# Expert tiles of a mixture-of-experts layer: two products on 128 stationary columns, or on four column tiles of 32

## The chip, the cores and the metric

One NeuronCore of a Trainium2 chip runs the whole program. The metric is the device time of one execution in microseconds, the median of several runs; lower is better. TensorE does the matrix products and transposes, ScalarE (ACT) and VectorE (DVE) take results out of the accumulators (PSUM), GpSimd (POOL) issues the gathers and scatters, and the queue SP issues nearly all other transfers.

## The reference

The input is 8 streams of 512 tokens with 128 features. Four parts follow one another, each added to its input: a four-layer attention encoder with dense feed-forward layers, a mixture of experts, a rotary attention layer, and the same mixture of experts again. The mixture is the part that the change touches:

```
top_v, top_i = jax.lax.top_k(routing_logits, TOP_K)          # 2 of 8 experts per token
...
h = gelu(jnp.einsum('bnd,edf->bnef', x, W1) + b1)             # D = 128, F = 512
y = jnp.einsum('bnef,efd->bned', h, W2) + b2
out = jnp.einsum('bne,bned->bnd', comb, y)
```

All of it is float32.

## The kernel before

The kernel doesn't compute all experts for all tokens. Tokens are sorted by chosen expert: each normalised token is scattered to two places of a list in memory (`x_rows`), each expert's part of the list is padded to a multiple of 256 rows, and the list is worked through in **tiles** of 256 rows of one expert. The first mixture is **round 0**, the second **round 1**; each has 46 tiles, in two groups of streams (23 and 23 in round 0, 31 and 15 in round 1).

One tile runs as follows. SP loads the expert's pack (both weights and biases, 578 KB) and the tile's 256 rows into one of six buffers. TensorE transposes the rows in two pieces of 128 (`rows_to_columns`, L779), ScalarE copies them out of PSUM (L937). `up` (L794) forms the four pieces of the hidden layer: the stationary operand is a 128 x 128 piece of W1, the moving one the 256 columns of the tile. ScalarE applies gelu with the bias (L952). `down` (L804) forms the result: for each half of 128 rows, four products with 128 stationary and 128 moving columns are accumulated. VectorE adds the bias (L1393), and SP stores the rows in `y_rows`. GpSimd later gathers each token's two rows (L1560), and VectorE adds them up with their weights (L1186).

The order on each engine is written out by hand. In a tile's first half TensorE does `up` of tile i and then the transposes of tile i+1; in its second half `down` of tile i-1. Between the halves, `tiles_order` puts other work: first the tail of the attention layer before (`tail`, 2 positions a half tile in round 0, 1.5 in round 1), and in round 0, once the first streams are combined, the head of the rotary attention layer (`head`, 2.45 positions a half tile). Where neither is left, the stream of TensorE is `up`, transposes, `down`, `up`, ... alone.

Nearly all products of the attention and dense layers go through the helper `mm4` (L482 to L485): it splits the 128 stationary columns into four column tiles of 32, issues one matmul for each, and writes 32 partitions of the result with each. In the profile these carry the line of the helper, L484, and the shape `128*32` (rows * columns of the stationary operand). The score products of the attention, L604 and L612, are written as column tiles as well, and L650 uses 9 columns of each. The transposes (L491, L668, L674, L779), the routing products and, before the change, both products of an expert tile use the full array, `128*128`. A product of float32 data appears in the trace as two pairs of weight load and matmul.

Of the kernel before, what the change touches and what calls it, by code (L numbers as in the profile page):

```python
# [27 lines left out]
P = 128  # L28
D = 128
# [5 lines left out]
FT = 4  # L35
# [35 lines left out]
TILE = 256  # L71
# [9 lines left out]
DEEP = 6  # L81
# [15 lines left out]
def hybrid_kernel(nc, x, apack, fpack, final, bpack, mpack, b2e, w1e, w2e,  # L97
                  alibi, rope, out, part_scr):
    ctx = ExitStack()
    with ctx:  # L100
# [3 lines left out]
        def sem(name):  # L104
            return ctx.enter_context(nc.semaphore(name))
# [34 lines left out]
        W1 = [pack[n][:, 0:FT * P] for n in range(DEEP)]  # L140
        W2 = [pack[n][:, FT * P:2 * FT * P].rearrange("p (f d) -> p f d", f=FT) for n in range(DEEP)]
# [5 lines left out]
        xcols = [rest[:, 768 + TILE * n:768 + TILE * (n + 1)] for n in range(2)]  # L147
        hT = [rest[:, 1280 + FT * TILE * n:1280 + FT * TILE * (n + 1)].rearrange("p (f t) -> p f t", f=FT) for n in range(2)]
# [54 lines left out]
        bankX, bankH = [bank[0], bank[4]], [bank[1:3], [bankPV, bankR]]  # L203
# [67 lines left out]
        eh_ready = sem("eh_ready")  # L271
# [195 lines left out]
        def beside(round_, i):  # L467

            return round_ == 0 and i >= FIRST[0]

        def one_bank(round_, i):

            return round_ == 0 and i >= FIRST[0] - 3

        def bank_of_results(round_, i):
            return bankY[0 if one_bank(round_, i) else (round_ * ETILES + i) % 2]

        @block.tensor
        def _(pe):
            mm = nc.tensor.matmul  # L480

            def mm4(out, stationary, moving, start=True, stop=True):  # L482
                for c in range(0, P, 32):
                    last = mm(out[c:c + 32], stationary[:, c:c + 32], moving, start=start, stop=stop)  # L484
                return last  # L485
# [296 lines left out]
            def up(round_, i):  # L782
                n = round_ * ETILES + i
                pe.wait_ge(exT_ready, n + 1)
                if i == FIRST[0] and round_ == 0:
                    jobs = ENC + round_ * JOBS
                    pe.wait_ge(slots_ready, JOBS * (round_ + 1))
                    pe.wait_ge(ot_done, QUADS * jobs)
                    pe.wait_ge(x_added, 2 * jobs - 1)
                    pe.wait_ge(f_added, 2 * ENC - 1)  # L790
                for ft in range(FT):
                    if n >= 1 and ft % 2 == 0:
                        pe.wait_ge(egelu_done, FT * (n - 1) + ft + 2)
                    mm(bankH[beside(round_, i)][ft // 2][:, (ft % 2) * TILE:(ft % 2 + 1) * TILE], W1[i % DEEP][:, ft * P:(ft + 1) * P],  # L794
                       xcols[n % 2], start=True, stop=True).then_inc(eh_ready, 1)

            def down(round_, i):
                n = round_ * ETILES + i
                pe.wait_ge(egelu_done, FT * (n + 1))
                if n >= 2:  # L800
                    pe.wait_ge(ey_added, n if one_bank(round_, i) else n - 1)
                for h in range(2):
                    for ft in range(FT):
                        last = mm(bank_of_results(round_, i)[:, h * D:(h + 1) * D], hT[n % 2][:, ft, h * P:(h + 1) * P],  # L804
                                  W2[i % DEEP][:, ft, :], start=(ft == 0), stop=(ft == FT - 1))
                last.then_inc(ey_ready, 1)

            def tile(round_, i, half_tile):
                if half_tile == 0:
                    if i == 0:  # L810
                        rows_to_columns(round_, 0)
                    up(round_, i)
                    if i + 1 < ETILES:
                        rows_to_columns(round_, i + 1)
                else:
                    if i >= 1:
                        down(round_, i - 1)
                    if i == ETILES - 1:
                        down(round_, i)
# [1050 lines left out]
```

## Time and profile before

| | |
|---|---|
| median of 3 runs | 2507.29 us (2502.47 to 2508.13) |
| profiled execution, first to last instruction | 2558.5 us; the page gives no time of its own beside the span |
| TensorE matmul busy | 2237.2 us (87%) |
| TensorE weight load busy | 1405.0 us (55%) |
| VectorE, ScalarE, GpSimd busy | 1764.9, 1442.5, 1042.2 us |
| mean granted TensorE clock | 0.933 |
| L794 (`up`), L804 (`down`): matmul busy | 188.4 and 185.9 us |

The share of a whole span is an average over stages. The tiles of round 0 lie between about 1575 and 1850 us, those of round 1 between 2310 and 2517 us; for those stretches the views by window and in order of time are of more use. In the timeline, a group's length reaches from its first start to its last modelled end; since matmuls are pipelined, the next group starts before that end, so the cost of a group is read from start to start.

### The profile page before, as it was taken

Reading aid. Unit: us, or ns where it says so; the run is one execution under the profiler, and the core shown is the slowest. Engines: PE = TensorE matmul, PEld = TensorE weight load, DVE = VectorE, ACT = ScalarE, POOL = GpSimd, SP = SyncE. Lnnn points to the kernel's source line nnn. Section 1 sums busy time; section 2 is a strip of 40 time slices with the busy share of each in tenths; the row PEclk is TensorE's granted clock in tenths of the full one; section 3 lists DMA queues with packets and bytes.
Section 4 is the critical chain, followed back from the end, with each engine's and each line's share of the span. In section 5 each row is a group of like instructions: output and inputs, shape, how many; then the busy total and the mean of one; then the engine's idle time right before and its main releaser. Section 6 shows DMA issues by size and latency. Waiting matters only on the chain.

```text
span 2558.5 us, 102575 instructions
## 1 busy us (share of the span) xinstructions
PE 2237.2 (87%) x44398; PEld 1405.0 (55%) x44398; DVE 1764.9 (69%) x5525; ACT 1442.5 (56%) x2646; POOL 1042.2 (41%) x1261
## 2 busy tenths in 40 slices
PE   2689999999999999999998888887888777888983
PEld 1345565656555656565555445786644444437872
DVE  6777888787878888888888774224677767852212
ACT  0257777777777777777755555342244434554441
POOL 6233434343434343434455554333244554452135
PEclk9789999999999999999988889999998888889997
DMA  4244433333433433433222203575522221206774
GB/s 117 82 137 118 128 117 123 114 124 113 127 117 116 130 107 119 125 121 110 78 68 69 83 25 107 166 227 161 150 62 66 62 68 60 61 18 194 218 211 111
DMA packets 162531, 288.76 MB, mean 113 GB/s; under 512 B 28504, under 2 KB 116312, under 8 KB 160344
## 3 DMA queue, kind: packets, MB, share of 16 engines
q1 hardware_dynamic: 153696, 264.23, 33.9%
q0 software_dynamic: 8384, 17.97, 2.6%
q8 instruction: 350, 5.73, 0.9%
q14 instruction: 101, 0.83, 0.1%
HBM read 227.33 MB, written 95.96 MB: 126 GB/s over the span
## 4 chain that ended last, share of the span: by engine, by line
PE 67%; DVE 14%; ACT 6%; issue 4%; POOL 3%; DMA 2%; another core or an unknown queue 2%; SPq 2%; POOLq 0%; ACTq 0%; DVEq 0%
PE bank L484 25%; PE bank L650 11%; PE bank L604 10%; PE bank L794 5%; DVE mx L1287 4%; PE bank L804 4%; PE bank L668 3%; PE bank L491 2%; ACT L915 1%; PE bank L612 1%; ACT big L885 1%; DVE xs L1186 1%; ACT fhT L915 1%; ACT OT L891 1%
## 5 line engine op out<-in xcount | busy, mean ns | idle before, releaser
L885 ACT ACTIVATE big<-bank 128x512 f32<-128x512 f32 x1600 | 900.2, 597 | 599.6 <-PE bank L484 518.5
L1287 DVE TENSOR_REDUCE mx<-bank 128x16 f32<-128x512 f32 (+1 forms) x1440 | 895.0, 653 | 290.5 <-PE bank L612 242.2
L1583 POOL TENSOR_SCALAR_AFFINE_SELECT big<-big 128x768 f32<-128x768 f32 (+1 forms) x640 | 397.6, 644 | 853.5 <-ACT big L885 853.4
L484 PE MATMUL bank<-QS,KS 99*32 99x128 bf16 (+3 forms) x10240 | 655.5, 312 | 32.4 <-ACT big L885 21.4
L604 PE MATMUL bank<-KS,QS 96*32 96x512 bf16 (+15 forms) x10240 | 592.9, 294 | 67.7 <-DVE mx L1287 40.0
L650 PE MATMUL bank<-big,V 128*9 128x512 f32 (+3 forms) x5120 | 445.3, 451 | 19.8 <-POOL big L1583 9.4
L604 PEld LDWEIGHTS bank<-KS,QS 96*32 96x32 bf16 x10240 | 249.9, 99 | 307.9 <-issue 155.1
L484 PEld LDWEIGHTS bank<-QS,KS 99*32 99x32 bf16 x10240 | 222.9, 99 | 201.0 <-ACT big L885 86.9
L612 PE MATMUL bank<-mask_a,ident_b 128*32 128x64 bf16 (+1 forms) x5760 | 309.6, 196 | 1.7 <-issue 1.7
L952 ACT ACTIVATE big<-bank,big 128x256 f32<-128x256 f32 x368 | 150.6, 471 | 247.7 <-PE bank L794 206.7
L650 PEld LDWEIGHTS bank<-big,V 128*9 128x9 f32 x5120 | 131.5, 92 | 167.9 <-issue 103.7
L1393 DVE TENSOR_TENSOR big<-bank,big 128x256 f32<-128x256 f32 x92 | 39.0, 424 | 255.9 <-PE bank L804 184.7
L794 PE MATMUL bank<-big 128*128 128x256 f32 x736 | 188.4, 401 | 24.2 <-ACT big L937 18.4
L804 PE MATMUL bank<-big 128*128 128x128 f32 x1472 | 185.9, 280 | 13.1 <-issue 10.0
L612 PEld LDWEIGHTS bank<-mask_a,ident_b 128*32 128x32 bf16 x5760 | 167.6, 99 | 38.1 <-issue 33.4
L804 PEld LDWEIGHTS bank<-big 128*128 128x128 f32 x1472 | 175.6, 195 | 18.5 <-issue 15.8
L794 PEld LDWEIGHTS bank<-big 128*128 128x128 f32 x736 | 140.1, 201 | 50.1 <-ACT big L937 21.4
L1568 POOL TENSOR_TENSOR resid<-qk,parts 128x512 f32<-128x512 f32 x80 | 96.5, 1206 | 170.8 <-DVE parts L1244 170.8
L1540 POOL DMA_INDIRECT x_rows<-xnR,slots x128 | 126.2, 986 | 59.9 <-issue 31.3
L484 PE MATMUL bank<-xnT,fp_sb 128*32 128x512 f32 x1024 | 133.1, 612 | 11.7 <-ACT fhT L915 11.6
L668 PE MATMUL bank<-ident,OT 128*128 128x128 f32 x640 | 109.4, 296 | 34.3 <-DVE attn L1328 31.6
L484 PE MATMUL bank<-fp_sb,fhT 128*32 128x128 f32 x4096 | 130.3, 273 | 0.2 <-ACT fhT L915 0.2
(216 smaller groups left out, 2732.0 us busy)
## 6 DMA issues: line engine op xcount, KB each, us to landing
big<-e_pack SPq DMA_DIRECT2D x92, 578.0 KB
QS<-part_scr SPq DMA_DIRECT2D x480, 96.0 KB
KS<-part_scr SPq DMA_DIRECT2D x480, 96.0 KB
part_scr<-parts SPq DMA_DIRECT2D x80, 384.0 KB
x_rows<-in_alibi SPq DMA_DIRECT2D x47, 384.0 KB, 4.8
y_rows<-in_alibi SPq DMA_DIRECT2D x47, 384.0 KB, 5.1
big<-x_rows SPq DMA_DIRECT2D x92, 128.0 KB
y_rows<-big SPq DMA_DIRECT2D x92, 128.0 KB
```

The lines of the kernel that those rows point to most:

```text
L484: last = mm(out[c:c + 32], stationary[:, c:c + 32], moving, start=start, stop=stop)
L604: mm(bk[h * SUB:(h + 1) * SUB, col:col + w], Q[0:ROW_MAX, 4 * quad + h, i * SUB:(i + 1) * SUB], K[0:ROW_MAX, 4 * quad + h, 0:w], start=(co ...
L612: last = mm(blocks[h * SUB:(h + 1) * SUB], ident_b[:, 0:SUB], mask, start=False, stop=True)
L650: last = mm(bankPV[32 * h:32 * h + HD + 1, kt * P:T], V[(b + j) % 3][:, kt, 4 * g + h, :], Pq[g % 2][:, h, KT_COL[kt]:KT_COL[kt] + T - kt ...
L668: last = nc.tensor.transpose(bankR[:, g * P:(g + 1) * P], OT[:, g, t * P:(t + 1) * P], ident[:])
L794: mm(bankH[beside(round_, i)][ft // 2][:, (ft % 2) * TILE:(ft % 2 + 1) * TILE], W1[i % DEEP][:, ft * P:(ft + 1) * P], xcols[n % 2], start= ...
L804: last = mm(bank_of_results(round_, i)[:, h * D:(h + 1) * D], hT[n % 2][:, ft, h * P:(h + 1) * P], W2[i % DEEP][:, ft, :], start=(ft == 0) ...
L885: A(dst, src, ACT.Exp).then_inc(exp_done, 1)
L952: A(hT[n % 2][:, ft, :], bankH[beside(round_, i)][ft // 2][:, (ft % 2) * TILE:(ft % 2 + 1) * TILE], ACT.Gelu, bias=B1[i % DEEP][:, ft:ft + ...
L1287: v.tensor_reduce(mx[:, quad, k, 0:w], src, axis=AX.X, op=ALU.max).then_inc(a_used, 1)
L1540: g.indirect_dma_start(out=x_rows, out_offset=bass.IndirectOffsetOnAxis(ap=slots[:, S % JOBS, c:c + 1], axis=0), in_=xnR[:, S % 2, c % TT, ...
L1583: g.affine_select(out=blocks, in_=blocks, compare_op=ALU.is_ge, fill=0.0, base=0, pattern=[[0, n], [1, P]], channel_multiplier=-1).then_in ...
```

## The change

Both products of an expert tile go through `mm4`: instead of one matmul with 128 stationary columns, four with 32 each are issued one after another. The moving operands, the accumulation over the hidden pieces, the waits and the semaphore increments are the same (the increment is on the last of the four). The transposes of the tile are unchanged.

```
-                    mm(bankH[beside(round_, i)][ft // 2][:, (ft % 2) * TILE:(ft % 2 + 1) * TILE], W1[i % DEEP][:, ft * P:(ft + 1) * P],
-                       xcols[n % 2], start=True, stop=True).then_inc(eh_ready, 1)
+                    mm4(bankH[beside(round_, i)][ft // 2][:, (ft % 2) * TILE:(ft % 2 + 1) * TILE], W1[i % DEEP][:, ft * P:(ft + 1) * P],
+                        xcols[n % 2]).then_inc(eh_ready, 1)
...
-                        last = mm(bank_of_results(round_, i)[:, h * D:(h + 1) * D], hT[n % 2][:, ft, h * P:(h + 1) * P],
-                                  W2[i % DEEP][:, ft, :], start=(ft == 0), stop=(ft == FT - 1))
+                        last = mm4(bank_of_results(round_, i)[:, h * D:(h + 1) * D], hT[n % 2][:, ft, h * P:(h + 1) * P],
+                                   W2[i % DEEP][:, ft, :], start=(ft == 0), stop=(ft == FT - 1))
```

The helper, which was there before:

```
            def mm4(out, stationary, moving, start=True, stop=True):
                for c in range(0, P, 32):
                    last = mm(out[c:c + 32], stationary[:, c:c + 32], moving, start=start, stop=stop)
                return last
```

## Rows read from the trace of the kernel before

**Rows 1.** Windows, L794 alone: window, its length, busy us (entries), clock, DMA share, GB/s.

```profile
1735.00:1850.00 115.00, 34.47 (x128) 25.09 (x128) 0.93 0.56 161
2310.00:2515.00 205.00, 91.34 (x368) 68.50 (x368) 0.97 0.70 204
```

**Rows 2.** Windows: busy us (entries) of PE, PEld, DVE, ACT, POOL; clock; DMA share; GB/s.

```profile
1735.00:1850.00 115.00, 101.06 (x1129) 76.81 (x1127) 61.98 (x160) 31.62 (x81) 34.33 (x34) 0.93 0.56 161
2310.00:2515.00 205.00, 186.29 (x1294) 168.75 (x1287) 42.98 (x178) 92.17 (x236) 57.18 (x59) 0.97 0.70 204
2410.00:2460.00 50.00, 50.00 (x352) 46.64 (x351) 5.76 (x14) 25.20 (x67) 2.47 (x3) 1.00 0.81 230
```

**Rows 3.** The chain that ended last, 2250 to 2560 us, shares by line.

```profile
by line: PE bank L794 27.1%; PE bank L804 22.2%; another core or an unknown queue 6.7%; PE bank L650 4.8%; POOL xnR L1560 4.5%; PE bank L484 4.3%; ACT big L885 3.6%; issue 3.6%; ACT big L952 3.4%; PE bank L779 2.9%; POOL fp_sb L1560 2.1%; P
```

**Rows 4.** Timeline of PE, one tile of round 1: start us, length us, engine, line, instruction.

```profile
2414.74 1.89 PE L794 MATMUL bank<-big 128*128 128x256 f32 x8
2416.46 0.38 PE L779 MATMUL bank<-ident,big 128*128 128x128 f32 x2
2416.68 1.95 PE L804 MATMUL bank<-big 128*128 128x128 f32 x16
2418.47 1.89 PE L794 MATMUL bank<-big 128*128 128x256 f32 x8
```

**Rows 5.** Timeline of PE, dense layer of the encoder in column tiles.

```profile
1005.43 1.92 PE L484 MATMUL bank<-xnT,fp_sb 128*32 128x512 f32 x16 [0.17 <-ACT fhT L915]
1007.17 0.29 PE L604 MATMUL bank<-KS,QS 96*32 96x256 bf16 x4
...
1008.18 1.94 PE L484 MATMUL bank<-fp_sb,fhT 128*32 128x128 f32 x64
1009.94 0.40 PE L604 MATMUL bank<-KS,QS 96*32 96x512 bf16 x4
```

**Rows 6.** Timeline of PE, rotary layer: column tiles, full-array transposes, column tiles.

```profile
1907.49 1.07 PE L484 MATMUL bank<-xnT,bp_sb 128*32 128x512 f32 x8 [0.70 <-DVE rtmp L1261]
1908.49 0.66 PE L668 MATMUL bank<-ident,OT 128*128 128x128 f32 x4
1909.08 0.29 PE L604 MATMUL bank<-KS,QS 96*32 96x256 bf16 x4
```

**Rows 7.** Timeline of PE, round 0: a tile between positions of the head.

```profile
1802.84 0.21 PE L612 MATMUL bank<-mask_a,ident_b 128*32 128x64 bf16 x4
1802.98 1.99 PE L794 MATMUL bank<-big 128*128 128x256 f32 x8
1804.81 0.38 PE L779 MATMUL bank<-ident,big 128*128 128x128 f32 x2
1805.12 0.40 PE L604 MATMUL bank<-KS,QS 96*32 96x64 bf16 x8
...
1806.48 0.20 PE L612 MATMUL bank<-mask_a,ident_b 128*32 128x64 bf16 x4
1806.62 2.05 PE L804 MATMUL bank<-big 128*128 128x128 f32 x16
1808.60 0.40 PE L604 MATMUL bank<-KS,QS 96*32 96x128 bf16 x8
1808.83 0.20 PE L612 MATMUL bank<-mask_a,ident_b 128*32 128x64 bf16 x4
1808.86 0.39 PE L604 MATMUL bank<-KS,QS 96*32 96x160 bf16 x8
```

**Rows 8.** Waits, 1655 to 1735 us: who waited for whom, us in total, times, longest.

```profile
POOL fp_sb L1560 <- DMA y_rows<-big: 28.1, 1, 28.1
```

**Rows 9.** The page, its first line.

```profile
span 2558.5 us, 102575 instructions
```

**Rows 10.** Windows of 10 us, columns as in rows 2.

```profile
190.00:200.00 10.00, 9.72 (x321) 7.12 (x313) 7.15 (x28) 6.61 (x12) 2.44 (x4) 1.00 0.81 202
1800.00:1810.00 10.00, 10.00 (x162) 7.80 (x162) 9.53 (x22) 1.92 (x5) 3.51 (x4) 1.00 0.82 219
```

## The prediction

> **What bounds the kernel now.** I read the stage windows first, to find where the changed lines run. L794 (first product of an expert tile) and L804 (second) leave 8 and 16 entries a tile. All 46 tiles of the second round lie in 2310 to 2515 us (368 entries of L794); of the 46 of the first round 16 lie in 1735 to 1850 us (128 entries), so 30 before that [rows 1]. The reader should see two kinds of stretch. In 2310 to 2515 us TensorE is busy 186.3 of 205 us, and from 2410 to 2460 it is busy 50.00 of 50.00 us at granted clock 1.00 (2.4 GHz), while the DMA share is 0.81 [rows 2]. The chain that ended last confirms it for 2250 to 2560 us: L794 and L804 hold 27.1% and 22.2% of it [rows 3]. So in the second round TensorE's own stream sets the pace; ScalarE, VectorE and the loads fit beside it.
>
> The timeline of one tile there shows what the stream consists of [rows 4]: start to start, 1.72 us for the first product (8 entries: four products, each in two passes because the data is f32), 0.22 us for the two transposes L779, 1.79 us for the second product (16 entries). Sum 3.73 us a tile, no gaps. A change helps only if it shortens these three numbers or the joints between them.
>
> **The change part by part.** Each matmul on 128 stationary columns becomes four on 32. A tile had 8 + 2 + 16 = 26 pairs of weight load and matmul; it will have 32 + 2 + 64 = 98. No wait, DMA or semaphore increment is added: the increment sits on the last of the four.
>
> *Streaming.* The dense layers already run this form with f32, so the price is in the trace. Two dense first-layer products of 512 columns (16 entries on 32 stationary columns) stream as many columns as the four of 256 in a tile: start to start 1.74 us [rows 5], against 1.72. The dense second layer has 64 entries of 128 columns in 1.76 us [rows 5], exactly the number and shape that a tile's second product will have, against 1.79. Up and down together: 3.50 against 3.51. The form itself gains and loses nothing (-0.01 us).
>
> *The joints.* The transposes stay on the full array, so each tile's stream now goes column tiles, full, column tiles. Such a joint can be read elsewhere: a 512-column f32 product in column tiles ahead of four full transposes takes 1.00 us to the next start instead of 1.74/2 = 0.87, so +0.13; the four transposes then take 0.59 us to the next column tile instead of the 0.43 that twice a tile's two come to, so +0.16 [rows 6]. Round trip 0.29 us. Nearer in place, but without the entry, is the exit from two L779 transposes to a column tile in the first round: 0.31 instead of 0.22, +0.09 [rows 7]. Entry 0.13 and exit 0.09 give the lower bound 0.22; 0.29 is the upper. I take 0.27, nearer to the upper because only that row has both halves around one short group. With the -0.01 above a tile alone costs +0.26 us (bounds 0.21 and 0.28): 3.73 becomes 3.99 us.
>
> *Where joints are saved.* From 1735 to 1850 us the first attention work of the next layer, in column tiles, is woven into both halves of a tile. There the tile pays now [rows 7]: entry to L794 0.14 us after the mask matmuls instead of about 0.03, +0.11, and L794 itself 1.83 instead of 1.72, +0.11; exit after L779 +0.09; entry to L804 again +0.11; L804 to the next column tile 1.98 instead of 1.79, +0.19. Sum 0.61 us. After the change only the transposes are left as a joint, 0.27: a saving of 0.34 us for each tile woven so. I count 26 such crossings from column tiles to full array in that part, two a tile, so 13 of its 16 tiles; the other 3 behave like lone tiles.
>
> *The sum.* Second round: 46 x 0.26 = +12.0 us, all on the path by [rows 2, 3]. First round before 1735 us: 30 tiles x 0.26 = +7.8 us, but the end of that part hangs on a gather that waited 28.1 us for stored rows [rows 8], so some is hidden behind it; I take +5. The woven part: -13 x 0.34 + 3 x 0.26 = -3.6 us; TensorE is busy 101.1 of 115 us there [rows 2], VectorE and the loads end several of its waits, so I take half, -1.8. Together +15 us, rounded down to +14 because the tail of the first round has some full-array neighbours that don't pay twice. The profiled execution spans 2558.5 us [rows 9], 51 us more than the 2507.3 us median of the three runs; the page gives no other time of its own for it, and the sum of differences is carried over to the median unchanged: 2507.3 + 14 = **2521 us** (2572 on the profile's span).
>
> Bounds of this case: 46 x 0.21 + 0 - 13 x 0.39 = +4.6 us if everything ahead of 1735 us is hidden and the woven part counts in full; 46 x 0.28 + 30 x 0.28 - 0 = +21.3 us if it is the reverse. So 2512 to 2529.
>
> The Trainium skill (TensorEngine Tiling (Array Packing), Key Properties) says that a change of tiling mode drains the array. Taken as a full drain, an estimate from [rows 4] is the tail by which a group outlasts the start of the next (1.89 against 1.73 us), so 0.16 a crossing and 0.33 a round trip, 0.32 a lone tile; the same four terms would then come to some +19 us in place of +14. The trace has the drain, with 0.29 at most, so it comes out a little cheaper than that.
>
> **The rivals.**
>
> *The crossings cost nothing around so short a group.* If the loads for the two transposes go in while the last column tiles still stream, the lone tile stays at 3.72 us and the woven tiles gain their full 0.61 us: 76 x -0.01 - 13 x 0.61 = -8.7 us, 2499 us, faster. It decides below about 0.05 us a round trip (76 x 0.05 = 3.8 against 8.7). For it: no row shows two transposes with column tiles on both sides. Against it: every entry and every exit that I found costs 0.09 to 0.16 [rows 6, 7]. Chance 0.05.
>
> *The loss is swallowed.* TensorE idles 18.7 of the 205 us of the second round [rows 2]. If those pauses end at times set by transfers, a later TensorE finds them shorter, and the second round loses perhaps a third of its 12 us, the first nothing, with the saving of 3.6 in full: about 2508 us, no change. For it: the DMA share of 0.81. Against it: in 2410 to 2460 us, the stretch with the highest share, TensorE never waits. Chance 0.13.
>
> *Issue or instruction supply becomes the bound.* A tile has 98 pairs where it had 26, about 246 in 10 us at 3.99 us a tile. In the tile stretches the most seen in 10 us is 162 pairs, with TensorE busy 10.00 [rows 10]; were that a ceiling, a tile would take 98/16.2 = 6.05 us, 2.3 us more, and 76 of them +176 us: 2683. Against it: early in the kernel 321 pairs went through in 10 us at the same DMA share, 0.81 and 0.82 [rows 10]. Chance 0.02 for this, and some 0.04 for small pauses of it that bring the total to 2530 to 2545.
>
> The Trainium skill (TensorE: Matmul & The Clock Gate, section "Wait — 56ns, not 53.3ns?") states about 62 ns per matmul where microcode issues it; 98 x 0.062 = 6.08 us a tile by that, the same outcome. The trace disagrees here: 64 pairs in 1.76 us are 27 ns each [rows 5].
>
> **How the numbers follow.** Crossings as priced: 0.76; swallowed 0.13; free crossings 0.05; issue 0.06. A measurement of this kernel tells about 0.2% (5 us) from no change. Slower by more: 0.76 x 0.95 + 0.06 = 0.78; within: 0.04 + 0.13 = 0.17; faster: 0.05. The range runs from 2508 (the swallowed case at its edge) to 2530 (the upper bound of the likeliest); left out are the free crossings, issue, and a part of the swallowed case, under 2 in 10.
>
> **What would show it.** In the profile after, the lone tile of the second round should go 1.74 + 0.13 us from first product to transposes, 0.31 to 0.36 us from transposes to second product, 1.76 us to the next tile: period 3.94 to 4.01 us. The products appear at the line inside the helper (L484) with 32 columns, 2944 and 5888 matmuls. Between 1735 and 1850 us the tiles should get shorter by about 0.3 us. The clock granted should stay at 1.00 in the dense part. Wrong would be: a period of 3.73 or less (crossings free), a period above 4.1 with TensorE waiting for nothing that the profile shows (issue), or a longer period with the same end, pauses shrunk (swallowed).

## The result and the profile after

| | before | after |
|---|---|---|
| median of 5 runs | 2507.29 us (2502.47 to 2508.14) | 2522.88 us (2519.50 to 2530.20, but for one run) |
| ratio of after to before | | 1.0067, 95% interval 1.0050 to 1.0085 |
| span of the profiled execution | 2558.5 us | 2520.3 us |

The kernel became slower: by 0.67% in the ratio, and by 15.6 us between the medians, where +14 us (2521 us) was forecast. One of the five runs after, 2912.70 us at a granted clock of 0.73 where the others have 0.93 to 0.94, was disturbed and is left out of the ratio.

The spans of the two profiles go the other way, so stages can't be read off them. The first profile of the kernel before holds pauses in which several engines stand still; a second profile of the same kernel (run e0 below) spans 2506.7 us, and stages are compared with that one. First the page of the changed kernel, then the same lines of e0:

```profile
span 2520.3 us, 115823 instructions
PE 2224.5 (88%) x51022; PEld 1332.6 (53%) x51022; DVE 1774.0 (70%) x5525; ACT 1442.9 (57%) x2646; POOL 1043.7 (41%) x1261
q8 instruction: 402, 6.59, 1.1%
```

```profile
span 2506.7 us, 102575 instructions
PE 2210.1 (88%) x44398; PEld 1392.3 (56%) x44398; DVE 1772.0 (71%) x5525; ACT 1442.8 (58%) x2646; POOL 1042.4 (42%) x1261
q8 instruction: 350, 5.73, 1.0%
```

TensorE has 6624 more pairs of weight load and matmul, 92 x 72 as counted in the prediction; nothing else has changed in number. The products of the tiles now stand at the helper's line, in the counts forecast; their busy time is 183.0 and 181.6 us against 183.6 and 182.9 in e0, so the form itself costs nothing:

```profile
L484 PE MATMUL bank<-big 128*32 128x256 f32 x2944 | 183.0, 390 | 1.1 <-ACT big L937 1.1
L484 PE MATMUL bank<-big 128*32 128x128 f32 x5888 | 181.6, 275 | 1.8 <-DVE big L1393 1.4 <-issue 0.4
```

The timeline of PE for a lone tile of the second round answers to [rows 4]. `down` and `up` follow each other at one line, so they are merged (96 entries):

```profile
2401.25 0.44 PE L779 MATMUL bank<-ident,big 128*128 128x128 f32 x2
2401.61 3.68 PE L484 MATMUL bank<-big 128*32 128x128 f32 x96
2405.22 0.44 PE L779 MATMUL bank<-ident,big 128*128 128x128 f32 x2
2405.59 3.68 PE L484 MATMUL bank<-big 128*32 128x128 f32 x96
```

Start to start: 0.36 to 0.37 us from the transposes to `down` (0.22 before), 3.61 us for `down` and `up` (3.51 before), period 3.98 us (3.73 before). Both additions lie at the two joints. The load side shows what is lost there. In e0 the weight load of a group starts ahead of its first matmul and hides behind the group before: 0.21 us ahead for the transposes (2402.06 against 2402.27 us) and 0.11 us for `down` (2402.38 against 2402.49):

```profile
2402.06 0.36 PEld L779 LDWEIGHTS bank<-ident,big 128*128 128x128 f32 x2
2402.38 1.86 PEld L804 LDWEIGHTS bank<-big 128*128 128x128 f32 x16
```

After the change it starts only with the matmul, 2401.24 against 2401.25 us and 2401.61 against 2401.61:

```profile
2401.24 0.20 PEld L779 LDWEIGHTS bank<-ident,big 128*128 128x128 f32 x2 [0.41 <-issue]
2401.61 3.20 PEld L484 LDWEIGHTS bank<-big 128*32 128x32 f32 x96 [0.17 <-ACT big L952]
```

The gelu (L952) that the second line names had ended at 2398.2 us for the tile in question, so ScalarE isn't what held that load. The idle 0.4 us before the transposes' load stands in each of 32 tiles between 2330 and 2460 us; e0 has no such wait there.

In the same window TensorE is busy without a gap in both kernels, at granted clock 1.00 (first e0, then after), so neither the clock nor a wait for another engine explains anything there:

```profile
2330.00:2460.00 130.00, 130.00 (x915) 121.14 (x914) 29.57 (x112) 67.09 (x175) 40.12 (x41) 1.00 0.83 239
```

```profile
2330.00:2460.00 130.00, 130.00 (x3221) 94.43 (x3217) 27.79 (x109) 61.70 (x162) 32.63 (x34) 1.00 0.81 232
```

A woven tile, as in [rows 7]:

```profile
1795.63 1.90 PE L484 MATMUL bank<-big 128*32 128x256 f32 x32
1797.46 0.44 PE L779 MATMUL bank<-ident,big 128*128 128x128 f32 x2
1797.83 0.40 PE L604 MATMUL bank<-KS,QS 96*32 96x64 bf16 x8
...
1799.22 1.92 PE L484 MATMUL bank<-big 128*32 128x128 f32 x64
1800.97 0.39 PE L604 MATMUL bank<-KS,QS 96*32 96x128 bf16 x8
```

Its parts are 1.83, 0.37 and 1.75 us, 3.95 together. In [rows 7] they were 1.83, 0.31 and 1.98 with 0.11 us of entry ahead of each product, 4.34. It saves 0.39 us.

The stages can be cut where VectorE adds the bias of a tile (L1393): first tile of the first round, tile 29, last tile of that round, first and last of the second. First e0, then after:

```profile
1576.17 0.42 DVE L1393 TENSOR_TENSOR big<-bank,big 128x256 f32<-128x256 f32 x1 [0.95 <-PE bank L804]
1724.14 0.42 DVE L1393 TENSOR_TENSOR big<-bank,big 128x256 f32<-128x256 f32 x1 [1.19 <-PE bank L804]
1830.22 0.42 DVE L1393 TENSOR_TENSOR big<-bank,big 128x256 f32<-128x256 f32 x1 [2.21 <-PE bank L804]
2293.28 0.42 DVE L1393 TENSOR_TENSOR big<-bank,big 128x256 f32<-128x256 f32 x1 [3.26 <-PE bank L804]
2465.79 0.42 DVE L1393 TENSOR_TENSOR big<-bank,big 128x256 f32<-128x256 f32 x1 [1.36 <-PE bank L804]
```

```profile
1578.91 0.42 DVE L1393 TENSOR_TENSOR big<-bank,big 128x256 f32<-128x256 f32 x1 [1.09 <-PE bank L484]
1733.16 0.42 DVE L1393 TENSOR_TENSOR big<-bank,big 128x256 f32<-128x256 f32 x1 [0.98 <-PE bank L484]
1836.79 0.42 DVE L1393 TENSOR_TENSOR big<-bank,big 128x256 f32<-128x256 f32 x1 [2.16 <-PE bank L484]
2297.04 0.42 DVE L1393 TENSOR_TENSOR big<-bank,big 128x256 f32<-128x256 f32 x1 [3.67 <-PE bank L484]
2480.47 0.42 DVE L1393 TENSOR_TENSOR big<-bank,big 128x256 f32<-128x256 f32 x1 [1.27 <-PE bank L484]
```

| stretch | e0 | after | difference | forecast |
|---|---|---|---|---|
| first round, first tile to tile 29 | 148.0 | 154.3 | +6.3 | +5 |
| first round, tile 29 to the last (woven) | 106.1 | 103.6 | -2.4 | -1.8 |
| second round, first to last tile | 172.5 | 183.4 | +10.9 | +12.0 |

The rest of the 13.6 us between the spans, -1.2 us, lies in stretches without a tile, where the two executions differ by up to 3 us in either direction.

### The profile page after: what moved, and what is told of

It reads as the page before. It is cut to its first block, busy times and chain, and to the rows that moved or that the text cites. A ratio compares the mean times of both kernels' runs of the same rounds, so it can differ in the third digit from the quotient of the medians.

```text
span 2520.3 us, 115823 instructions
## 1 busy us (share of the span) xinstructions
PE 2224.5 (88%) x51022; PEld 1332.6 (53%) x51022; DVE 1774.0 (70%) x5525; ACT 1442.9 (57%) x2646; POOL 1043.7 (41%) x1261
## 4 chain that ended last, share of the span: by engine, by line
PE 64%; DVE 16%; POOL 5%; ACT 5%; issue 4%; DMA 4%; SPq 2%; POOLq 0%; ACTq 0%; DVEq 0%
PE bank L484 33%; PE bank L650 11%; PE bank L604 10%; DVE mx L1287 5%; PE bank L668 3%; PE bank L491 2%; ACT L915 2%; PE bank L612 1%; POOL x_rows L1540 1%; ACT big L885 1%; DMA KS<-part_scr 1%; DVE xs L1186 1%; DMA y_rows<-big 1%; PE bank L779 1%; ACT OT L891 1%
## 5 line engine op out<-in xcount | busy, mean ns | idle before, releaser
L484 PE MATMUL bank<-QS,KS 99*32 99x128 bf16 (+3 forms) x10240 | 647.4, 311 | 21.4 <-ACT big L885 16.2
L604 PE MATMUL bank<-KS,QS 96*32 96x512 bf16 (+15 forms) x10240 | 586.1, 293 | 86.1 <-DVE mx L1287 46.3
L650 PE MATMUL bank<-big,V 128*9 128x512 f32 (+3 forms) x5120 | 437.5, 451 | 20.3 <-POOL big L1583 14.3
L484 PE MATMUL bank<-big 128*32 128x128 f32 (+1 forms) x8832 | 352.2, 314 | 2.9 <-DVE big L1393 1.4
L484 PEld LDWEIGHTS bank<-big 128*32 128x32 f32 x8832 | 250.2, 111 | 74.7 <-issue 13.7
L952 ACT ACTIVATE big<-bank,big 128x256 f32<-128x256 f32 x368 | 151.0, 470 | 231.5 <-PE bank L484 231.3
L1393 DVE TENSOR_TENSOR big<-bank,big 128x256 f32<-128x256 f32 x92 | 38.8, 423 | 225.0 <-PE bank L484 203.9
L668 PE MATMUL bank<-ident,OT 128*128 128x128 f32 x640 | 109.4, 296 | 32.7 <-DVE attn L1328 30.2
L1449 POOL TENSOR_TENSOR rstd<-veps,mhalf 128x4 f32<-128x4 f32 x80 | 81.1, 1014 | 106.4 <-DVE veps L972 103.6
L1560 POOL DMA_INDIRECT fp_sb<-y_rows,slots x80 | 77.2, 964 | 106.1 <-DVE big L1393 49.4
```

The lines of the kernel that those rows point to most:

```text
L604: mm(bk[h * SUB:(h + 1) * SUB, col:col + w], Q[0:ROW_MAX, 4 * quad + h, i * SUB:(i + 1) * SUB], K[0:ROW_MAX, 4 * quad + h, 0:w], start=(co ...
L650: last = mm(bankPV[32 * h:32 * h + HD + 1, kt * P:T], V[(b + j) % 3][:, kt, 4 * g + h, :], Pq[g % 2][:, h, KT_COL[kt]:KT_COL[kt] + T - kt ...
L668: last = nc.tensor.transpose(bankR[:, g * P:(g + 1) * P], OT[:, g, t * P:(t + 1) * P], ident[:])
L952: A(hT[n % 2][:, ft, :], bankH[beside(round_, i)][ft // 2][:, (ft % 2) * TILE:(ft % 2 + 1) * TILE], ACT.Gelu, bias=B1[i % DEEP][:, ft:ft + ...
L1449: g.tensor_tensor(rstd[:], veps[:], mhalf[:], ALU.pow).then_inc(done, 1)
```

## The experiments

The theory: what costs is the crossing between column tiles and full array, once there and once back around the transposes, some 0.25 us a tile, and the column form costs nothing. The rival: each converted product costs by its own entries. A second rival: the number of instructions. Times of one kernel differ by several us from run to run (the kernel before: 2493 to 2519 us over 27 runs), so the period of a lone tile, which repeats to 0.01 us, decides where it can.

**e0, the kernel before once more**, unchanged, for a profile.

> The kernel before once more, for a profile without the pauses in which all engines stand still that the first profile has (its span is 51 us above the median of its runs). Theory: the same 3.73 us a lone tile and 4.3 us a woven one, with a span near 2505 us, so that the stages can be set against those of the changed kernel: the second round some 11 to 12 us shorter than after the change, the first 3 to 6 us. Rival (the pauses belong to the kernel): a span near 2555 us again.

Measured, in one run: 2508.43 us, span 2506.7 us, period 3.73 to 3.74 us. The second round differs from the changed kernel by 10.9 us, where 11 to 12 were expected, the first by 3.9 us up to its last tile. The pauses of the first profile didn't come back.

**e1, only `up` through the helper; e2, only `down`.** In e1 the first of these two edits stands alone, in e2 the second:

```
-                    mm(bankH[beside(round_, i)][ft // 2][:, (ft % 2) * TILE:(ft % 2 + 1) * TILE], W1[i % DEEP][:, ft * P:(ft + 1) * P],
+                    mm4(bankH[beside(round_, i)][ft // 2][:, (ft % 2) * TILE:(ft % 2 + 1) * TILE], W1[i % DEEP][:, ft * P:(ft + 1) * P],
...
-                        last = mm(bank_of_results(round_, i)[:, h * D:(h + 1) * D], hT[n % 2][:, ft, h * P:(h + 1) * P],
+                        last = mm4(bank_of_results(round_, i)[:, h * D:(h + 1) * D], hT[n % 2][:, ft, h * P:(h + 1) * P],
```

> Only the first product of an expert tile in column tiles, the second on the full array. Theory (what costs is the crossing between column tiles and full array, not the form): a lone tile still has one round trip, now around the first product instead of around the transposes, so its period is 3.95 to 4.02 us as with the whole change (3.98), against 3.73 before; in the woven part only the joint from the attention work to the first product is saved. Total 2507 + 11.5 + 5 = about 2523 us, as much as the whole change or a little more. Rival (each product converted costs by its own entries): a third of the entries, so a third of the loss, period 3.81, about 2512 us.

> Only the second product in column tiles, the first on the full array. Theory (crossings): again one round trip in a lone tile, period 3.93 to 4.00 us; in the woven part the two joints around the second product are saved, so it is a little better there than the first product alone: about 2519 to 2522 us. Rival (entries): two thirds of the loss, period 3.90, about 2517 us; so the two halves of the change would add up to the whole, where by the theory each costs the whole.

Timeline of PE in e1:

```profile
2400.57 1.93 PE L484 MATMUL bank<-big 128*32 128x256 f32 x32
2402.44 0.44 PE L779 MATMUL bank<-ident,big 128*128 128x128 f32 x2
2402.71 1.95 PE L804 MATMUL bank<-big 128*128 128x128 f32 x16
2404.59 1.93 PE L484 MATMUL bank<-big 128*32 128x256 f32 x32
```

and in e2:

```profile
2401.79 1.95 PE L484 MATMUL bank<-big 128*32 128x128 f32 x64
2403.68 1.99 PE L794 MATMUL bank<-big 128*128 128x256 f32 x8
2405.51 0.38 PE L779 MATMUL bank<-ident,big 128*128 128x128 f32 x2
2405.82 1.96 PE L484 MATMUL bank<-big 128*32 128x128 f32 x64
```

The period is 4.02 us in e1 and 4.03 us in e2; the rival had 3.81 and 3.90. Adding a third or two thirds of the pairs costs slightly more than adding them all (3.98); e2 lies 0.03 us above the 3.93 to 4.00 that were expected. The parts can now be told apart: entry to the full array 0.13 us (`up` 1.87 instead of 1.74 in e1; `down` 1.89 instead of 1.76 in e2) and then 0.05 to 0.11 us in the first full group (transposes 0.27 instead of 0.22 in e1, `up` 1.83 instead of 1.72 in e2); exit 0.09 us (transposes 0.31 in e2, `down` 1.88 instead of 1.79 in e1). From first to last tile the second round takes 184.6 and 184.7 us. In all, e1 took 2516.41 us (ratio 1.0044, 1.0022 to 1.0066), e2 2522.06 us (1.0061, 1.0039 to 1.0083). e1 is 7 us below its forecast of 2523; the difference isn't in the second round, where its profile is 1.2 us longer than that of the whole change, but its first 30 tiles took 150.0 us against 154.3. The whole change's 1.0067 lies at the edge of e1's interval.

**e3, two round trips a tile; e8, the same splitting on the full array.** The two transposes are issued apart, one in the middle of `up` and one behind it; e3 starts from the changed kernel, e8 from the one before.

```
                 for ft in range(FT):
+                    if ft == 2 and i + 1 < ETILES:
+                        rows_to_columns(round_, i + 1, (0,))
...
-                        rows_to_columns(round_, i + 1)
+                        rows_to_columns(round_, i + 1, (1,))
```

> The changed kernel with the two transposes of a tile apart, one in the middle of the first product and one behind it: same instructions, two round trips a tile instead of one. Theory: a second 0.25 us in every lone tile, period 4.20 to 4.27 us, and in the woven tiles as well, 92 x 0.25 = 23 us less what is hidden: about 2540 us (2534 to 2548). Rival (entries, or issue): nothing changes, about 2523 us.

> The kernel before (full array) with the same splitting of the two transposes that cost the changed kernel a second round trip. Theory (crossings): there is no column tile next to them in a lone tile, so the splitting itself costs nothing: 3.73 to 3.78 us a lone tile, 2505 to 2511 us. Rival (splitting costs by itself, by the earlier wait for the rows or the two short groups): some 0.3 us a tile here as well, about 2528 us.

Timeline of PE in e3, one period:

```profile
2400.51 1.07 PE L484 MATMUL bank<-big 128*32 128x256 f32 x16
2401.51 0.33 PE L779 MATMUL bank<-ident,big 128*128 128x128 f32 x1
2401.77 2.82 PE L484 MATMUL bank<-big 128*32 128x128 f32 x80
2404.52 0.33 PE L779 MATMUL bank<-ident,big 128*128 128x128 f32 x1
2404.78 1.07 PE L484 MATMUL bank<-big 128*32 128x256 f32 x16
```

and in e8:

```profile
2404.05 1.03 PE L797 MATMUL bank<-big 128*128 128x256 f32 x4
2404.92 0.27 PE L779 MATMUL bank<-ident,big 128*128 128x128 f32 x1
2405.03 1.03 PE L797 MATMUL bank<-big 128*128 128x256 f32 x4
2405.90 0.27 PE L779 MATMUL bank<-ident,big 128*128 128x128 f32 x1
2406.01 1.95 PE L807 MATMUL bank<-big 128*128 128x128 f32 x16
2407.79 1.03 PE L797 MATMUL bank<-big 128*128 128x256 f32 x4
```

A second crossing, with the same instructions in another order, lifts the period from 3.98 to 4.27 us (+0.29); on the full array the same splitting leaves it at 3.74. In all e3 took 2539.78 us (1.0132, 1.0098 to 1.0165), as forecast, and e8 2511.68 us (1.0017, 0.9997 to 1.0037), 0.7 us above its forecast and at the edge of what can be told from no change. The crossing is the cause.

**e4, the transposes in column tiles too; e7, the same in tiles of 64; e6, products alone in tiles of 64.** In e4 and e7 the two transposes become products with the identity, through the helper (in the trace two pairs for each f32 product). In e6 and e7 a helper with two tiles of 64, `mm2`, takes the place of `mm4` in the expert tiles.

```
-                    last = nc.tensor.transpose(bankX[beside(round_, i)][:, h * P:(h + 1) * P], xrows[i % DEEP][:, h, :], ident[:])
+                    last = mm4(bankX[beside(round_, i)][:, h * P:(h + 1) * P], xrows[i % DEEP][:, h, :], ident[:])
...
+            def mm2(out, stationary, moving, start=True, stop=True):
+                for c in range(0, P, 64):
+                    last = mm(out[c:c + 64], stationary[:, c:c + 64], moving, start=start, stop=stop)
+                return last
```

> The changed kernel with the tile's two transposes as products with the identity in column tiles, so that a lone tile has no crossing left; as f32 products they take two passes each. Theory: no joints, 1.74 + 0.43 + 1.76 = 3.93 us a lone tile against 3.98 with the change, transposes 0.43 us instead of 0.37 plus the entry: about 2519 us (2516 to 2522). Rival (entries or issue set the pace): 112 pairs a tile instead of 98, 4.15 us or more, about 2533 us.

> Both products in two column tiles of 64 instead of four of 32: half the entries, the same number of crossings in a lone tile, but now also a crossing to and from the attention work in tiles of 32. Theory (crossings): a lone tile takes 3.95 to 4.0 us as with four, and the woven tiles lose their saving: 2523 to 2528 us. Rival (entries): half the loss, period 3.85, about 2515 us. If a change from 64 to full costs less than one from 32 to full, the period lies between as well; then the time from transposes to second product tells it.

> As the run with column transposes, but products and transposes in two tiles of 64: no crossing in a lone tile, 56 pairs of entries a tile instead of 112. In the run before, the lone tile took 3.91 us as the crossings said, but TensorE paused for nothing that the profile shows, and each pause came about 128 pairs behind the one before. Theory (those pauses are the supply of instructions, 256 of which fill one 16 KB packet of the instruction queue): at half the entries they are gone, period 3.91 us throughout, second round 7 to 9 us shorter than with 112 pairs (182 to 184 us from first to last tile), while the woven tiles cross between 64 and 32 columns as before: about 2520 us in all. Rival (the pauses come from the column transposes themselves, such as a late accumulator): they stay, round two about 190 us, in all about 2530 us.

In e6 the tile has half the entries and the same joints, and the same period: 3.99 us (2402.95 to 2406.94 us in the lines below). It took 2523.46 us (1.0055, 1.0029 to 1.0081). The number of entries is no part of the change's loss.

```profile
2402.95 0.43 PE L784 MATMUL bank<-ident,big 128*128 128x128 f32 x2
2403.32 3.69 PE L489 MATMUL bank<-big 128*64 128x128 f32 x48
2406.94 0.44 PE L784 MATMUL bank<-ident,big 128*128 128x128 f32 x2
```

Among the attention work e6 shows one thing more. There its tiles of 64 meet tiles of 32, and that crossing costs too: `down` starts 0.13 us behind the start of the mask matmuls (1803.56 to 1803.69 us) and takes 1.90 us to the next tile of 32 (1805.59), where the changed kernel has 0.03 and 1.75. The woven stretch took 107.1 us against 103.6 after the change, so the saving is gone, as expected.

In e4 the joints are gone and the median period is 3.91 us, near the 3.93 expected; yet the whole took 2530.65 us (1.0081, 1.0056 to 1.0107) where 2519 was expected. Timeline of PE, products and transposes at one line, of a stretch where tiles took about 5 us:

```profile
2404.60 1.36 PE L484 MATMUL bank<-big 128*32 128x128 f32 x39
2406.91 2.59 PE L484 MATMUL bank<-big 128*32 128x128 f32 x56 [0.95 <-issue]
2409.29 0.65 PE L484 MATMUL bank<-ident,big 128*32 128x128 f32 x16
2409.72 1.73 PE L484 MATMUL bank<-big 128*32 128x128 f32 x55
2412.20 2.24 PE L484 MATMUL bank<-big 128*32 128x128 f32 x41 [0.75 <-issue]
```

TensorE pauses for nothing that the profile shows; between two pauses lie 56 + 16 + 55 = 127 pairs, 254 instructions. The instruction queue q8 moved 52 packets more in the changed kernel than in e0 for 13,248 more instructions: 255 a packet. So these two pauses lie one packet apart; the next three, at 2471 to 2482 us, follow each other after 127 and 126 pairs. From first to last tile of the second round there are 6 pauses with 6.0 us in all. e7, with half the entries and no joints either, has none of them there: TensorE's longest wait among its lone tiles is 0.3 us, for VectorE, and the median period is 3.91 us. But e7 changes the width of the tiles together with the number of pairs, so it doesn't settle the cause alone. From first to last tile the second round took 190.5 us in e4 and 181.7 us in e7, and e7 2519.26 us in all (1.0045, 1.0021 to 1.0069).

**e5, column tiles only where the head is woven in** (tiles 30 to 45 of the first round).

```
+            def woven(round_, i):
+                return round_ == 0 and i >= 30
...
+                    (mm4 if woven(round_, i) else mm)(bankH[beside(round_, i)][ft // 2][:, (ft % 2) * TILE:(ft % 2 + 1) * TILE], W1[i % DEEP][:, ft * P:(ft + 1) * P],
...
+                        last = (mm4 if woven(round_, i) else mm)(bank_of_results(round_, i)[:, h * D:(h + 1) * D], hT[n % 2][:, ft, h * P:(h + 1) * P],
```

> Column tiles only in the 16 tiles of the first round among which the head of the rotary layer is woven; all others on the full array as before. Theory: the lone tiles keep 3.73 us, and 13 tiles save 0.34 us each, 4.4 us if all of it is on the path, half if half is: 2503 to 2506 us, faster by 0.05 to 0.2%. Rival (the form itself costs, wherever it is used): 16 x 0.25 = +4 us, about 2511 us.

Measured 2504.88 us, ratio 1.0002 (0.9982 to 1.0021), 12 runs. The lone tiles have 3.73 us again and the woven ones the short joints, but the woven stretch takes 105.6 us against 106.1 in e0, and 103.9 in e8, which has no column tile there. So a gain of some 2 us can neither be shown nor excluded. Part of a gain was lost again: TensorE's busy time in that stretch fell from 90.1 us in e0 to 87.7, but 3.1 us of pauses came in for which the profile shows no wait, the longest 2.5 us. Two of them, at 1803.39 and 1807.37 us, lie 127 pairs apart like those of e4, here without a transpose in column tiles. In the same stretch the changed kernel has 1.0 us of such pauses and e0, e1, e2 and e8 have none.

## Why the prediction was right

*The form costs nothing.* Right: 3.50 us were read off the dense layers for `up` and `down`, and e4 and e7, without joints, run 3.91 us a tile with 0.43 us of transposes as products in it, 3.48 without these.

*A round trip costs 0.27 us.* Right: 3.98 - 3.73 = 0.25 against 0.26 forecast, 0.29 for the second one in e3. The two rows that priced it, +0.13 in and +0.09 to +0.16 out [rows 6, 7], return in e1 and e2 one by one. The lower bound of 0.22 left out the 0.05 to 0.11 us that the first full group behind the entry loses there. The Trainium skill (TensorEngine Tiling (Array Packing), Key Properties) says that changing the tiling mode drains the array; the trace agrees in that every crossing costs, 0.25 to 0.29 us a round trip, below the 0.33 that the prediction estimated for a full drain. The profiles show that the weight load doesn't run ahead across a crossing; whether it is a drain that holds it back, no run here shows.

*Where it counts in full.* Right: from first to last tile the second round grew by 10.9 us, 45 periods at 0.25 being 11.3.

*Where it is half hidden.* +6.3 us measured for the first 30 tiles against +5. This term is less sure than the number looks: e1 and e2, with the same lone period, show 150.0 and 148.0 us there against 148.0 in e0. TensorE's busy time there grew by 7.5 us, near the 7.8 of the prediction, but the place of the hiding isn't the gather that it named. What shrank are TensorE's own waits, for VectorE's normalised rows (L979) and a load of an expert pack above all: 14.3 us in e0, 13.1 after, and 9.3 and 8.6 in e1 and e2. How much reaches the end in a run isn't settled.

*The woven tiles.* The mechanism is right, 0.39 us saved a tile against 0.34 forecast, but its effect on the end, -2.4 us against -1.8, is within what that stretch varies by (e5, e8).

*The last 1 us.* The reason for rounding 15 down to 14, full-array neighbours that don't pay twice, was wrong. Where full-array work of the attention layer also stands behind `down`, a tile pays two round trips: with the transposes L668 there, `up` to `up` takes 4.71 us in e0 (1571.70 to 1576.41 us) and 5.14 us after (1574.22 to 1579.36), +0.43. That the total came out within 2 us is partly luck: the two halved terms, +5 and -1.8, were chosen without a row that gives the half, and single runs of one kernel differ by more.

*The rivals.* Crossings aren't free (3.98 us), and the loads for the transposes don't go in while column tiles stream. Nothing was swallowed in the second round. The 18.7 us of idle time that this rival built on were nearly all pauses of the one profiled execution; in e0 TensorE idles 0.5 us between the first and the last tile of that round. The supply of instructions, which got 0.06, did no harm to lone tiles of 98 pairs, but pauses that would fit it came at 112 (e4) and, to 1.0 us, in the woven stretch of the changed kernel. That rival was nearer than the 321 pairs in 10 us of [rows 10] made it look.

## What to carry to other kernels

Splitting a full f32 product into column tiles left its streaming time here as it was; price instead the places where TensorE changes between column tiles and the full array, some 0.25 us there and back in this kernel, and count them in the order in which the queue meets them. Converting only part of the work doesn't lower such a cost in proportion, and may raise it (e1, e2). Where work in column tiles is woven in, the same conversion removes crossings, so the sign can differ from stage to stage of one kernel.

## What the runs showed that was not expected

With 112 pairs of load and matmul in 3.91 us, TensorE paused 0.4 to 1.7 us at a time in the second round without a wait that the profile shows, several times 126 or 127 pairs apart. The transfers took 76% of the DMA engines' time between 2330 and 2460 us. At 98 pairs in 3.98 us (share 0.81) and at 56 pairs in 3.91 us (share 0.78) it didn't pause so in the lone stretch of the second round. That a late packet of instructions is the cause is argued from the spacing, in e4 and e5, and from e7, not shown directly, and why 321 pairs in 10 us went through at a share of 0.81 early in the kernel [rows 10] stays open.

The first profile of the kernel before was 51 us longer than its timed runs and another profile of it 1 us shorter than the median of them; two tiles of the second round that followed the one before by 8.7 and 14.3 us at L1393 in the first did so by 3.7 us in the second. Had the stages of the first profile been set against those after, the change would have looked like a gain of 12 us in the second round.
